# Loads ordered by first use and a shared table made by two engines in the first attention; eight gathers in flight and two sums in the second experts

## What is computed

```
qp, kp = elu(q) + 1, elu(k) + 1
kv  = einsum('bhsd,bhse->bhde', kp, v)
z   = einsum('bhsd,bhd->bhs', qp, kp.sum(axis=2))
out = (einsum('bhsd,bhde->bhse', qp, kv) / (z + EPS)) @ o_w.T + o_b
```

```
topk_idx, topk_w = _router(x, router_w, e_bias)
...                                   # slots_token, slots_w: (32, 80) by order of the tokens
Xp = x[slots_token].reshape(E, C, d)
Y  = einsum('eci,eid->ecd', silu(Xp @ W_gate) * (Xp @ W_up), W_down)
out = zeros((T, d)).at[slots_token].add(Y.reshape(EC, d) * slots_w[:, None])
return out + silu(x @ shared_gate.T) * (x @ shared_up.T) @ shared_down.T
```

## Time and profile before

| | us |
|---|---|
| median of 3 runs | 3708.29 |
| the profiled execution | 3726.15 |
| its span | 3724.2 |
| PE busy in the span | 3146.6 (84%) |
| first attention: first product on PE | at 50.80 |
| experts (`l1f`): first SP instruction to the first of `l2a` | 1221.08 to 1484.08 |
| of these the loop, first to last scatter issued | 1332.19 to 1467.59 |

### The profile page before, as it was taken

The page is one execution under the profiler, slowest core; times in us unless marked ns, Lnnn a source line. Parts: engine busy times, 40 slices in busy tenths (PEclk is TensorE's granted clock), DMA queues, the critical chain, the costliest instruction groups (busy, mean ns, idle before and its releaser), DMA issues. The chain is left out here.

```text
span 3724.2 us, 68279 instructions
## 1 busy us (share of the span) xinstructions
PE 3146.6 (84%) x23000; PEld 2342.1 (63%) x23000; DVE 2408.1 (65%) x5727; ACT 1700.8 (46%) x3204; POOL 1472.5 (40%) x1654
## 2 busy tenths in 40 slices
PE   4969969779999665795776999899999788888698
PEld 3747755359999443463555666577777566666565
DVE  3557744745555601784885888677777577777688
ACT  1337743435555221463673333344444455555376
POOL 2112224212222444554772785344444344443232
PEclk9979989679999755797997999999999999999799
DMA  3000010000000342000004000000000000000001
GB/s 117 1 20 14 12 61 6 1 3 4 3 3 2 99 103 58 5 6 23 14 15 174 18 18 12 2 1 0 0 0 0 4 2 2 2 2 1 20 25 37
DMA packets 83387, 82.69 MB, mean 22 GB/s; under 512 B 40415, under 2 KB 73983, under 8 KB 81794
## 3 DMA queue, kind: packets, MB, share of 16 engines
q1 hardware_dynamic: 78594, 74.80, 6.5%
q0 software_dynamic: 4608, 5.57, 0.9%
HBM read 63.96 MB, written 9.31 MB: 20 GB/s over the span
## 5 line engine op out<-in xcount | busy, mean ns | idle before, releaser
L1495 PE MATMUL bank<-far,l3a_ln_xnT 128*128 128x512 f16 x1152 | 271.5, 381 | 1.8 <-POOL l3a_ln_xnT L1311 1.8
L508 PE MATMUL bank<-l2f_xnT,l2f_wi 128*88 128x512 f16 x960 | 221.9, 381 | 1.5 <-DVE l2f_h L354 1.1
L1495 PEld LDWEIGHTS bank<-far,l3a_ln_xnT 128*128 128x128 f16 x1152 | 113.2, 98 | 111.3 <-issue 2.9
L1783 POOL TENSOR_TENSOR l3x_rr<-l3x_ss,minus_half 128x4 f32<-128x4 f32 x128 | 127.1, 1008 | 121.9 <-DVE l3x_ss L1627 121.9
L1789 POOL TENSOR_TENSOR l1x_prob<-l1x_prob,l1x_srec 128x512 f32<-128x512 f32 x64 | 66.6, 1041 | 262.0 <-DVE l1x_srec L1604 262.0
L508 PEld LDWEIGHTS bank<-l2f_xnT,l2f_wi 128*88 128x88 f16 x960 | 114.6, 120 | 81.1 <-issue 2.2
L367 DVE SCALAR_TENSOR_TENSOR x_res<-bank,l3f_combine,x_res 128x256 f32<-128x256 f32 x320 | 132.7, 477 | 24.8 <-PE bank L518 22.9
L1719 ACT ACTIVATE l3a_v<-bank 128x512 f32<-128x512 f32 x64 | 38.3, 598 | 226.7 <-PE bank L1495 226.7
L1773 POOL TENSOR_TENSOR l3a_q_tok<-l3a_qa,l3a_qb 128x512 f32<-128x512 f32 x64 | 81.5, 1274 | 143.5 <-DVEq L1618 143.5
L367 DVE SCALAR_TENSOR_TENSOR x_res<-bank,l2f_combine,x_res 128x256 f32<-128x256 f32 x320 | 132.6, 475 | 6.5
L2124 PE MATMUL bank<-l0x_v,l0x_pT 128*128 128x128 f32 x1024 | 133.9, 279 | 3.2 <-ACT l0x_pT L2539 1.5
(11 more groups left out here) (704 smaller groups left out, 9494.7 us busy)
## 6 DMA issues: line engine op xcount, KB each, us to landing
far<-in_l1f_in SPq DMA_DIRECT2D x32, 256.0 KB, 3.3
far<-in_l1f_down SPq DMA_DIRECT2D x32, 128.0 KB, 3.6
l2f_wi<-in_l2f_in SPq DMA_DIRECT2D x20, 176.0 KB
far<-l0x_kT SPq DMA_DIRECT2D x64, 48.0 KB
far<-l2x_kT SPq DMA_DIRECT2D x32, 96.0 KB
l3f_wi<-in_l3f_in SPq DMA_DIRECT2D x20, 128.0 KB
l3f_wd<-in_l3f_down SPq DMA_DIRECT2D x20, 128.0 KB
sums<-near SPq DMA_DIRECT2D x1, 2176.0 KB, 16.2
```

Source lines behind the costliest of these rows:

```text
L508: last = nc.tensor.matmul(bank[g % 2][0:width, :], wi16[u][p][:, a, k, :], xnT[q][:, k, 512 * g:512 * g + 512], start=(k + p + q == 0), st ...
L1495: last = nc.tensor.matmul(bank[:, 0:width], norm.xnT[u][q][:, k, :], w(k, at, width, p), start=(k + p + q == 0), stop=(k == KD - 1 and p = ...
L1783: nc.gpsimd.tensor_tensor(rr[:, at], ss[:, at], core.minus_half[:, 0:HC], ALU.pow).then_inc(rr_ready, 1)
```

## The change

**The start and the first attention.** The input x is loaded in four groups, each with its own semaphore. The start loads the identity, then group 0, and waits only for the identity. The rest moves into the first attention's SP list: the table, the first 2 of 17 steps of indices, the weights of this attention, its bias tables, then group 1, indices of 5 steps, groups 2 and 3, indices of 10 steps, the other small weights, and the zeros. `moments(b)` waits for its group. The entries are made by DVE (first halves) and ACT (second halves) instead of POOL. The bias rows are made after them instead of before the moments of block 0.

```diff
-                sp.dma_start(core.x[:, :, :], x_in.rearrange("b p d -> p b d")).then_inc(loaded, 16)
-                sp.dma_start(core.ident[:, :], ident_in).then_inc(loaded, 16)
...
-                sp.wait_ge(loaded, 32)
+                sp.dma_start(core.ident[:, :], ident_in).then_inc(core.ident_in, 16)
+                load_rows(sp, 0)
...
             def _(sp):
-                decode.load(sp)
+                decode.load_table(sp)
+                decode.load(sp, 0)
+                fetch(sp)
                 for i in range(2):
                     sp.dma_start(bias[i:i + 1, :], tables["bias"]).then_inc(tables_in, 16)
                 sp.dma_start(own_head[:, :], tables["own_head"]).then_inc(tables_in, 16)
                 sp.dma_start(out_bias[:, :], tables["out_bias"].partition_broadcast(P)).then_inc(tables_in, 16)
+                core.load_rows(sp, 1)
+                decode.load(sp, 1)
+                core.load_rows(sp, 2)
+                core.load_rows(sp, 3)
+                decode.load(sp, 2)
+                for fetch_ in later:
+                    fetch_(sp)
...
-    def make_entries(self, pool):
+    def make_first_halves(self, dve):
         nc = self.nc
+        dve.wait_ge(self.table_loaded, 16)
+        nc.vector.tensor_scalar(self.table[:, :], self.table[:, :], W_SCALE, None, ALU.mult)
+        dve.drain()
+        nc.vector.tensor_copy(self.table_hi[:, :], self.table[:, :])
+        dve.drain()
+        nc.vector.tensor_tensor(self.rest[:, :], self.table[:, :], self.table_hi[:, :], ALU.subtract
+                                ).then_inc(self.rest_ready, 1)
         for j in range(self.ENTRIES):
...
+            last = nc.vector.tensor_scalar(self.entry[j][0][:, :], self.core.ident[:, :], self.table[:, j:j + 1], None,
+                                           ALU.mult)
+        last.then_inc(self.entries_ready, 1)
+
+    def make_second_halves(self, act):
+        act.wait_ge(self.rest_ready, 1)
+        for j in range(self.ENTRIES):
+            last = self.nc.scalar.activation(self.entry[j][1][:, :], self.core.ident[:, :], ACT.Copy,
+                                             scale=self.rest[:, j:j + 1])
+        last.then_inc(self.entries_ready, 1)
```

```diff
-    RING, FETCH = 19, 4
+    RING, FETCH = 19, 8
...
                 def scatter(e):
                     pool.wait_ge(ey_kept, e + 1)
-                    if e >= 1:
-                        pool.wait_ge(added_in, 16 * e)
-                    nc.gpsimd.indirect_dma_start(sums, bass.IndirectOffsetOnAxis(index[1][:, e:e + 1], 0),
+                    if e >= 2:
+                        pool.wait_ge(added_in[e % 2], 16 * (e // 2))
+                    nc.gpsimd.indirect_dma_start(sums[e % 2], bass.IndirectOffsetOnAxis(index[1][:, e:e + 1], 0),
                                                  y[e % 3][:, :], None, compute_op=ALU.add
-                                                 ).then_inc(added_in, 16)
+                                                 ).then_inc(added_in[e % 2], 16)
...
+                    for i in range(2):
+                        sp.dma_start(back[b // 2 % 2][:, b % 2, i, :], sums[i][P * b:P * b + P, :]
+                                     ).then_inc(back_in[b % 4], 16)
...
+                for b in range(0, NB, 2):
+                    add_first(b)
+                    add_first(b + 1)
+                    dve.drain()
+                    add_second(b)
+                    add_second(b + 1)
...
                 for f in range(2 * NG):
+                    if f == 5:
+                        count()
+                    if f == 7:
+                        table()
                     up(f)
                     if f >= 2:
                         down(f - 2)
```

More of the change, by code:

```diff
@@ L925, in _ @@
                 dve.drain().then_inc(indexed, 1)
+                hidden(7)
                 for e in range(E):
@@ L1154, in down, with count, table @@
                     last.then_inc(y_made, 1)
+                def count():
+                    pe.wait_ge(sel_ready, 1)
+                    every = sel16.rearrange("p b e -> p (b e)")
+                    nc.tensor.matmul(b_pos[:, 0:NB * E], below16, every, start=True, stop=False)
+                    for d in range(1, NB):
+                        last = nc.tensor.matmul(b_pos[:, E * d:NB * E], ones16, every[:, 0:E * (NB - d)],
+                                                start=False, stop=(d == NB - 1))
+                    last.then_inc(counted, 1)
+                def table():
+                    pe.wait_ge(named_ready, 1)
+                    for b in range(NB):
+                        if b == 0:
+                            pe.wait_ge(at_ready, 1)
+                        elif b == NB // 2:
+                            pe.wait_ge(at_ready, 2)
+                        for k in range(K):
+                            last = nc.tensor.matmul(b_table[0:C, 0:E], at_pos[:, b, k, :], named[:, b, k, :],
+                                                    start=(b + k == 0), stop=(b == NB - 1 and k == K - 1))
+                    last.then_inc(tabled, 1)
                 for f in range(2 * NG):
+                    if f == 5:
+                        count()
+                    if f == 7:
+                        table()
                     up(f)
```

139 lines of the change are left out of this document (66 added, 73 removed).

## The result

The changed kernel takes 3647.97 us, the median of 4 runs (3632.45 to 3648.85). Beside it on the same chip the kernel before took 3708.45 (3704.83 to 3710.58, 4 runs).

The account below looks back on a forecast made before the run. Taken as bounds: load order and POOL's entries at the start, a scatter-gather-PE chain in the experts loop. Profiled 3726.15 - 32.9 - 46.5 + 7.4 = 3654.2, less 17.9 to the median: 3636 us, range 3612 to 3666.

Parts of the forecast that it names:

- First attention: Start: loads ordered by first use, entries made by DVE and ACT; first product at 17.9 instead of 50.80 us, -32.9.
- Router: Second experts layer before the loop: 14 us won at the count lost again in POOL's queue; first gather +0.9 us.
- (b): Rival, router: moved counts pay, if `named` were not behind `add_shared(1)`; -10 more, 3626 us; chance 0.12.
- First gather to PE: Start of the experts loop: weights issued earlier, so the first gather reaches PE in 2.8 instead of 5.3 us, -2.5.
- Loop: Experts: 24 at POOL's 2.95 us, last seven at PE's 2.82; -46.5 together with the start of the loop.
- the 1.97: Experts loop: time per scatter if two chains overlap, each scatter 3.93 us behind the one before it.
- its 13.8: Last seven expert turns at 1.97 us if PE's clock reaches 2.4 GHz, instead of 19.7; left out of the sum.
- End: Read-back of two arrays, two DMAs and two additions per block: 19.6 instead of 12.2 us, +7.4.
- everything twice: Upper end for the read-back of two arrays: 21.9 us.
- (a): Rival, experts loop: two scatters in flight overlap in nothing, one every 3.93 us; -15.2 instead of -46.5, 3668 us; chance 0.13.
- (c): Rival, experts loop: the eight gathers do nothing and the turn stays at 4.37 us; 3681 us; chance 0.05.
- (d): Rival, experts loop: indirect DMAs of one queue go one after the other; slower, +21.6, 3730 us; chance 0.04.

Follow-up runs that it names:

- e1: Kernel before with only the first attention's part (new load order, entries by DVE and ACT, bias rows), old experts: 3692.16 us, ratio 0.9931.
- e5: Changed kernel with the count, the table, `hidden(5)` and `hidden(7)` back in their old places: 3641.18 us, one run.
- e6: Changed kernel with only `named` moved ahead of `add_shared(1)` on POOL: 3634.25 us, one run.
- e9: Changed kernel with `named` ahead of `add_shared(1)`, four gathers ahead of the additions of groups 2 and 3, read-back in 8 DMAs: 3629.14 us, ratio 0.9755.
- e11: e9 with the counts and table back in their old place and `hidden_half(7)` ahead of the gathers: 3629.66 us, one run.
- e3: Kernel before with eight gathers in flight instead of four, still one array of sums: 3713.76 us, ratio 0.9999.
- e8: Changed kernel with four filling products per turn of `l1a`, two in each of PE's two pauses: 3631.44 us, ratio 0.9768.
- e0: The changed kernel again, nothing altered: 3649.59 us, ratio 0.9821.
- e7: Changed kernel with its layer `l1a` executed six times in a row, which changes the output: 4490.34 us.

## Why the prediction was right

**First attention, forecast -32.9 (first product at 17.9).** Right: 17.14, and -34.0 at the end of the layer. The identity landed a microsecond earlier than taken, and the layer started at 3.51 instead of 5.6. The bias tables, which were said to hold nothing up, cost 1.31 of it. e1 shows the term alone.

**Router, forecast first gather 99.2 and first scatter 109.5 behind the layer's start.** Right, and for the reason given: `named` at 77.5 (75.4 to 77.5 in four traces of this code; forecast 75.6), first gather 98.6 to 100.7, first scatter 108.6 to 110.6. The gathers ran up against POOL's `add_shared(3)`, as the path said. e5 shows that the moved counts change nothing measurable; e6, e9 and e11 show that it is POOL's order that holds them. Rival (b), the counts pay, had the place right and the condition too narrow: with `named` moved alone (e6) the first scatter comes 4 us earlier, not 10, because the gathers still stand behind the additions of groups 2 and 3.

**First gather to PE, forecast 2.8 instead of 5.3.** 1267.48 to 1270.47, 3.0.

**Loop, forecast 90.5.** 87.4, and for 24 turns the mechanism as told: POOL idles 0.30 between instructions, 2.95 per expert. The two parts were off in opposite directions, 3.1 and 6.2 us, so that the sum came within 3.1 is partly luck. The first 24 turns took 73.9 (1277.45 to 1351.38) and not 70.8, since two scatters waited for ACT's `y`, 2.0 and 1.1 us over the 2.95. The last seven took 13.5 (1351.38 to 1364.88) and not 19.7. Here the prediction had the wrong bound: it took PE's 2.82 per turn. First the windows of these turns in the changed kernel and in e9, then their rows in the changed kernel:

```profile
1351.38:1364.88 13.50, 7.90 (x37) 6.25 (x35) 0.95 (x4) 4.20 (x13) 9.80 (x7) 0.75 0.35 45
1358.38:1372.34 13.96, 10.27 (x39) 7.71 (x38) 0.95 (x4) 4.09 (x13) 9.80 (x7) 0.50 0.35 44
```

```profile
1355.23 1.39 POOL L1033 DMA_INDIRECT sums<-l1f_y,l1f_to_row  x1 [0.70 <-ACT l1f_y L1103]
...
1359.08 1.39 POOL L1033 DMA_INDIRECT sums<-l1f_y,l1f_to_row  x1 [0.58 <-ACT l1f_y L1103]
...
1358.42 0.47 ACT L1103 ACTIVATE l1f_y<-bank,l1f_got 80x256 f32<-80x256 f32 x1 [0.85 <-DMA sums<-l1f_y,l1f_to_row]
```

Scatters two apart, which go to the same array, follow each other after 3.85 to 4.11 us, near the 3.93 of the earlier trace rows. As in e3 their rows name ACT's `y`, and ACT itself had been released by a landing. So the two chains of scatters are the bound, the 1.97 that the prediction named and did not use for its value. PE had run ahead of them while POOL was the bound: its last product for an expert ended at 1360.37, 4.5 us before the last scatter. The speed of PE does not decide: in e9 PE was at 1.2 GHz in these turns (granted clock 0.50), and they took 13.96 us. The Trainium skill (TensorE: Matmul & The Clock Gate, "What's actually happening") says that activity releases the throttle, and the prediction had its 13.8 for these turns by that rule. The number came out, but not for that reason: at a granted clock of 0.75 and 0.50 these turns were not run at 2.4 GHz throughout, and by e9 they need not be.

**End, forecast +7.4.** +9.2 (21.35): near the 21.9 of "everything twice", 1.8 above the value.

**Rivals (a), (c), (d).** (a) had scatters 3.93 apart; two in flight overlap, as 2.95 shows. One array does give about that distance (e3). Its 3668 lies 2 us outside the range that was said to touch it. (c), eight gathers do nothing, is nearly true of them alone (-7.3 in the loop, nothing in the runs) and not with two arrays. (d), indirect DMAs one after the other, appears nowhere.

**The step that was off: from the profiled execution to the median.** The prediction subtracted 17.9 us because the profiled execution lay that far above the median of its runs, and took this for a constant of the measurement. It was `l1a`: 167.2 us in that trace. The two layers gave 73.2 us, where 72.0 were forecast, but the medians differ by 60.5 only. The value came out 12 low because the changed kernel's runs mostly lie near 3648 while its profiled one was at the short end. With `l1a` filled (e8) they all lie at 3627 to 3632. That the kernel before was mostly at the short length is likely by its runs, but only one of them has a trace. Whether the change makes a long `l1a` more frequent is open. If each run's time less the "without `l1a`" of its kernel's trace is taken for its `l1a`, an estimate good to some 5 us, 11 of the 15 runs of the changed kernel, e0 and e1 had more than 164 us, and 11 of the 38 of the kernel before beside the experiments.

## What to carry to other kernels

When a loop has two chains of nearly equal length, either fix alone looks useless (here -7 and -5 us in the loop, about what the same loop varies by, and nothing or worse in the total), and both together are worth 48: work out each chain's period from rows before dropping an edit that brought nothing. When an instruction is moved forward and nothing comes earlier, read the list of the engine that its result has to pass; the move may pay later, when that list is put in order (nothing measurable and then 12 us). And before a difference of half a per cent is ascribed to a change, compare the layers that the change does not touch.

## What the runs showed of the hardware that was not expected

One layer's length varied between 150.1 and 169.2 us from trace to trace with the same code, at a granted clock between 0.67 and 1.00, with 0.85 and 0.91 us of pause on PE in each turn in either case. In stretches of 10 us, a clock that had come down to 0.67 stayed at 0.66 or 0.67 for five to eight stretches, until near the layer's end (before, e0 to e6, e9); in after and e11 it came down to 0.70 and 0.69 once and went back to 1.00. The three lengths go with it: 167.0 to 169.2 us where it came down after some 60 us of the layer, 157.7 to 157.9 where after some 80, 150.1 where it went back. In e7 six executions in a row were long. Four more products per turn, which compute nothing, made it shorter and steady.
